# Adding four expert rows per token: engine sums against accumulating loads in a two-layer Mamba/attention + mixture-of-experts kernel

## The reference

```
xn = layernorm(x)                                   # layer 0
x  = x + ssd_block(xn) + moe(xn, 16 experts, top 4) + shared_expert(xn)
xn = layernorm(x)                                   # layer 1
x  = x + spike_attention(xn) + moe(xn, 8 experts, top 2)
```

## Time and profile before

| what | us |
|---|---|
| median of three runs | 2404.99 |
| the profiled execution, its own time | 2406.89 |
| its span in the trace | 2405.1 |
| bridge, first load issued to last normalized group | 1693.9 to 1796.2 |
| busy in the span: PE, DVE, ACT, POOL | 2187.2, 1595.0, 1190.7, 1435.2 |

### The profile page before, as it was taken

The page is one execution under the profiler, slowest core; times in us unless marked ns, Lnnn a source line. Parts: engine busy times, 40 slices in busy tenths (PEclk is TensorE's granted clock), DMA queues, the critical chain, the costliest instruction groups (busy, mean ns, idle before and its releaser), DMA issues. The chain is left out here.

```text
span 2405.1 us, 40728 instructions
## 1 busy us (share of the span) xinstructions
PE 2187.2 (91%) x12292; PEld 1586.7 (66%) x12292; DVE 1595.0 (66%) x3484; ACT 1190.7 (50%) x2677; POOL 1435.2 (60%) x1278
## 2 busy tenths in 40 slices
PE   4787999999999999999999989999288879999997
PEld 2455777777777777777777767777144656666665
DVE  4747888888888888888888845666687742222222
ACT  2356777777777777777777722222132341111111
POOL 1224777777777777777777756777643214444443
PEclk9898999999999999999999999999689899999999
DMA  7926454545545455454544448664540046222221
GB/s 255 359 83 146 139 151 132 152 139 151 149 132 156 136 154 145 133 156 139 153 143 132 141 139 278 191 218 150 202 157 1 1 166 173 46 44 45 45 43 20
DMA packets 195651, 330.34 MB, mean 137 GB/s; under 512 B 49267, under 2 KB 137588, under 8 KB 195188
## 3 DMA queue, kind: packets, MB, share of 16 engines
q1 hardware_dynamic: 139044, 233.43, 32.8%
q0 software_dynamic: 26880, 53.64, 8.8%
q10 hardware_dynamic: 29520, 40.66, 5.4%
HBM read 240.72 MB, written 87.84 MB: 137 GB/s over the span
## 5 line engine op out<-in xcount | busy, mean ns | idle before, releaser
L1006 DVE SCALAR_TENSOR_TENSOR m_cv<-m_hp,conv,m_cv 128x256 f32<-128x256 f32 x864 | 417.0, 483 | 112.2 <-ACT m_cv L905 91.0
L1397 PE MATMUL e_u<-wup,e_xgT 128*128 x1152 | 421.4, 499 | 9.0 <-issue 4.9
L1335 ACT ACTIVATE e_sil<-e_u 128x128 f32<-128x128 f32 (+1 forms) x216 | 82.9, 384 | 551.5 <-PE e_u L1397 524.5
L832 POOL TENSOR_TENSOR m_er<-m_er,m_cT 128x1024 f32<-128x1024 f32 x128 | 302.2, 2361 | 44.1 <-DVE m_ar L1013 44.1
L943 ACT ACTIVATE m_ar<-m_ar,m_ta 128x128 f32<-128x128 f32 x1024 | 318.7, 390 | 0.8
L1094 PE MATMUL m_hp<-xnT,wpj 128*128 128x259 f32 x1152 | 304.3, 387 | 7.8 <-PEq L144 4.5
L1397 PEld LDWEIGHTS e_u<-wup,e_xgT 128*128 128x128 f32 x1152 | 203.1, 191 | 141.3 <-issue 130.3
L1102 PE MATMUL m_gp<-xnT,wpj 128*128 128x256 f32 x1024 | 269.1, 385 | 11.2 <-ACT m_gT L923 11.2
L1094 PEld LDWEIGHTS m_hp<-xnT,wpj 128*128 128x128 f32 x1152 | 214.2, 192 | 68.8 <-issue 27.1
L1292 POOL DMA_INDIRECT out<-e_y,target x72 | 113.0, 1570 | 228.7 <-DVE e_y L1366 192.9
L839 POOL TENSOR_TENSOR m_hdd<-m_hdt,m_tb 128x512 f32<-128x512 f32 x128 | 131.0, 1043 | 193.8 <-DVE m_hdt L1021 193.8
(11 more groups left out here) (305 smaller groups left out, 3965.8 us busy)
## 6 DMA issues: line engine op xcount, KB each, us to landing
m_ar<-acum_rows_dram SPq DMA_DIRECT2D x512, 128.0 KB
m_er<-eacum_rows_dram SPq DMA_DIRECT2D x128, 512.0 KB
rows_by_slot<-blank_rows ACTq DMA_DIRECT2D x1, 18576.0 KB, 79.1
e_xg<-rows_by_slot ACTq DMA_DIRECT2D x132, 129.0 KB
m_xrow<-xn_rows SPq DMA_DIRECT2D x32, 512.0 KB
b_work<-y_rows SPq DMA_DIRECT2D x16, 1024.0 KB, 7.0
wup<-in_w SPq DMA_DIRECT2D x8, 1024.0 KB
wpj<-in_w_proj SPq DMA_DIRECT2D x1, 4352.0 KB, 24.4
```

What stands on the lines that cost most here:

```text
L832: g.tensor_tensor(er[:, t], er[:, t], middle(cT[:, t * P:(t + 1) * P], HQ), ALU.mult).then_inc(scaled.sem, 1)
L1006: v_.scalar_tensor_tensor(o, hp[n % 2][:, j:j + BLK], conv[:, c, j:j + 1], o, ALU.mult, ALU.add).then_inc(tapped.sem, 1)
L1397: ins = nc.tensor.matmul(u_ps[a.slot(2)][b][:, 0:width], xgT[:, a.slot(2), c, :], wup[:, c, ds(e * (2 * f) + b * width, width)], start=c = ...
```

## The change

The four rows are no longer loaded beside the stream and summed. GpSimd issues, for each group and each of the four choices, one DMA that reads that choice's rows (128 partitions x 4 pieces of 1 KB) and adds them into `xs` in SBUF as it lands. The four loads of a group follow each other, each waiting for the one before; groups are staggered, so that up to four groups are in progress. The sums on POOL (L1611, L1613), the addition on DVE (L1801) and SP's loads (L1582) are gone; DVE waits for the four landings of a group instead. The zeroing of `cmp` and the index tiles stand after the 32 loads in POOL's stream.

```diff
-        yg = work[:].rearrange("p (r t k d) -> p r t k d", r=2, t=BIG, k=K0)
...
-        s_yg = [sem(f"b_experts{n}") for n in range(4)]
+        s_yg = [sem(f"b_experts_added{n}") for n in range(NG)]
...
             @block.sync
             def _(sp):
-                def y_half(h):
-                    g, half = divmod(h, 2)
-                    if g >= 2:
-                        sp.wait_ge(s_x, g - 1)
-                    sp.dma_start(yg[:, g % 2, half * 2:half * 2 + 2].rearrange("p t k d -> p t (k d)"),
-                                 tokens(by_token, g * BIG + half * 2, 2)).then_inc(s_yg[h % 4], 16)
-
-                for h in range(4):
-                    y_half(h)
                 for g in range(NG):
-                    if g + 2 < NG:
-                        y_half(2 * g + 4)
-                        y_half(2 * g + 5)
                     sp.wait_ge(s_xn, g + 1)
...
             @block.gpsimd
-                for h in range(2 * NG):
-                    g, half = divmod(h, 2)
-                    pool.wait_ge(s_yg[h % 4], (h // 4 + 1) * 16)
-                    a = yg[:, g % 2, half * 2:half * 2 + 2]
-                    g_.tensor_tensor(a[:, :, 0:2, :], a[:, :, 0:2, :], a[:, :, 2:4, :], ALU.add).then_inc(s_pc, 1)
-                    pool.wait_ge(s_pc, h + 1)
-                    g_.tensor_tensor(a[:, :, 0, :], a[:, :, 0, :], a[:, :, 1, :], ALU.add).then_inc(s_ys, 1)
-                    if h == 1:
-                        (iotas and casts of tokid, ji, slot_row)
-                pool.wait_ge(s_x, NG - 1)
+                def add_choice(g, j):
+                    if j:
+                        pool.wait_ge(s_yg[g], 16 * j)
+                    pool.dma_start(xs[:, g * BIG:(g + 1) * BIG, :], tokens(by_token, g * BIG, BIG)[:, :, j * D:(j + 1) * D],
+                                   accum_op=ALU.add).then_inc(s_yg[g], 16)
+
+                for n in range(NG + K0 - 1):
+                    for j in range(K0 - 1, -1, -1):
+                        if 0 <= n - j < NG:
+                            add_choice(n - j, j)
                 g_.memset(cmp, 0.0).then_inc(s_cz, 1)
+                (iotas and casts of tokid, ji, slot_row)
...
             @block.vector
-                        dve.wait_ge(s_ys, 2 * s.n + 2)
-                        v.tensor_tensor(xs[:, at, :], xs[:, at, :], yg[:, s.n % 2, :, 0, :], ALU.add).then_inc(s_x, 1)
-                        dve.wait_ge(s_x, s.n + 1)
+                        dve.wait_ge(s_yg[s.n], 16 * K0)
```

More of the change, by code:

```diff
@@ L1543, in bridge_phase @@
         plane = lambda r, g: raw[:, r, ds(g * GT, GT)] if r < R - KD else xnT[:, r - (R - KD), ds(g * GT, GT)]
-        s_yg = [sem(f"b_experts{n}") for n in range(4)]
-        s_ys, s_pc = sem("b_y_summed"), sem("b_y_pairs")
-        s_x, s_lst, s_small, s_std0, s_rstd, s_xn = (sem("b_" + n) for n in (
-            "stream", "row_stats", "row_moments", "row_std", "row_rstd", "xn_done"))
+        s_yg = [sem(f"b_experts_added{n}") for n in range(NG)]
+        s_lst, s_small, s_std0, s_rstd, s_xn = (sem("b_" + n) for n in (
+            "row_stats", "row_moments", "row_std", "row_rstd", "xn_done"))
         s_row = [sem(f"b_rows_stored{n}") for n in range(XN)]
@@ new lines, in _ @@
+                g_.memset(cmp, 0.0).then_inc(s_cz, 1)
+                g_.iota(tokid[:], pattern=[[P, T]], base=-S, channel_multiplier=1).then_inc(s_iota, 1)
+                g_.iota(ji[:], pattern=[[1, 1]], base=0, channel_multiplier=1).then_inc(s_iota, 1)
+                g_.iota(slot_row_i[:], pattern=[[1, P]], base=0, channel_multiplier=0).then_inc(s_iota, 1)
+                pool.wait_ge(s_iota, 3)
+                g_.tensor_copy(token_f[:], tokid[:]).then_inc(s_turn, 1)
+                g_.tensor_copy(jf[:], ji[:]).then_inc(s_turn, 1)
@@ L1624, in _ @@
+                g_.tensor_copy(slot_row[:], slot_row_i[:]).then_inc(s_turn, 1)
                 g_.memset(mask[:], 1.0).then_inc(s_m, 1)
```

## The result

The changed kernel takes 2420.7 us (median of 8 runs, 2414.8 to 2424.0) against 2405.9 us for the kernel before in the same comparison. The ratio is 1.0057, 95% interval 1.0043 to 1.0072: slower by 0.6%, about 14 us. I had forecast slower, but by 87 us.

A forecast was written before the change was run, and what follows sets the result against it. Bound: the feed chain load, sum, normalize, up to the eighth group's addition. Last landing 1877.8 instead of 1791.5 us, +86.3; PE -1.1 and +2.2; sum +87.4 on the profiled 2406.9 us; against the median, 2492 us. Range 2425 to 2532.

The forecast's parts named there:

- What bounds the bridge: Between 1693.9 and 1797 us: the feed chain of load, sum, normalize sets the time, and PE comes last.
- GpSimd's price of an issue: POOL's own time for each new accumulating load: 0.40 us plus 1024 reads at 4.6 ns, 5.1 us.
- The DMA engines' price: Engine time per added 1 KB packet: 0.105 to 0.154 us, so 3.4 to 4.9 us per load.
- The pace: Spacing of the 32 loads: set by POOL's issue, 5.1 + 0.3 us, so 5.4 us per load.
- rival A: Bridge loads paced by the DMA engines at 3.4 to 4.9 us each: total about 2426 to 2474 us, chance 0.26.
- what I cost at nothing: Zeroing of `cmp` and index tiles behind POOL's loads, SP's row stores, DVE's slow tiny operations: no effect on the total.
- Three lone round trips: At the ends of the load stream: three loads are waited for alone, 3 x (5.1 + 4) = 27.3 us.
- PE's terms: PE at the eighth group: no longer late, -1.1 us; lower clock after gaps in transposes and projection, +2.2 us.
- The work moved behind the loads: Zeroing of `cmp` (1.8 us) and index tiles on POOL: covered before routing begins; without cover about 4 us.
- Rival D: Bridge loads: only the second read costs, 0.085 us per KB, 2.7 us per load; total 2403 us, chance 0.04.

## Why the prediction was wrong, point by point

* **What bounds the bridge:** right. All the loss lies between the first load and the eighth group's statistics. From there to the first gather of the last phase it is 0.9 us less than before: 1.2 us more to the kept scores, and 2.1 us less behind them, where I had expected no change.
* **GpSimd's price of an issue, 5.1 us: this step failed.** The trace after has 1.28 us for 512 pieces. I had read the surplus of the indirect adding DMA over the indirect plain one, 0.59 us, as 4.6 ns for each additional read, and then scaled it by the number of pieces. Measured on direct loads, 128 adding pieces cost 0.865 us, 512 cost 1.282 us, and the plain load, which goes out as 128 packets, 0.748 us: 1.1 ns per piece and a fixed part of about 0.7 us. The bounds of my sum went from 1.57 to 6.3 us, and the truth lay below the lower one. An indirect DMA's time was not a floor for a direct one.
* **The DMA engines' price, 0.105 to 0.154 us per added KB:** as the time of a packet right at its lower end, 0.104 us; as a pace too high. I multiplied it by the 32 pieces of an engine and got 3.4 us, as if the packets stood one behind the other. They overlap: full engines deliver a load in 2.7 us at a share of 1.23. The higher row held one DMA alone, with its start and its end; with a filled queue the row from the middle of a DMA was the nearer one.
* **The pace:** I took GpSimd's 5.4 us per load; the engines' 3.1 us (12.4 us per group over 4) decided. This was rival A, to which I gave 0.26. Its formula with the measured numbers, 29 x 3.1 + 3 x (1.28 + 1.2 + 3.1), gives 106.6 us against the 110.3 measured. Its lower end stood at 3.4 us per load, hence 2426 us, and that was also the lower end of my range; the overlap of the packets is what carried the time below it. That 3.4 and 3.1 are so near is partly luck. The overlap was left out, 0.7 us too much, and so were the row stores on the same engines, some 0.3 us too little: under "what I cost at nothing" I had asked only whether anybody waits for them.
* **Three lone round trips:** right in place. The first load alone took 6.3 us to landing, and the last pair shows 8.8 us between two issues (1788.23 to 1797.02). The size was 6.1 to 8.8 us (the last load is issued at 1797.02 and used at 1803.10) instead of 9.1.
* **PE's terms, -1.1 and +2.2 us:** the sum is right by luck. From the statistics of the eighth group to its kept scores it is 22.7 us (1803.10 to 1825.81) against 21.5 us before (1791.49 to 1813.03), +1.2 for +1.1 forecast. But PE was as late as before: it took up the group 5.9 us after the statistics began in both kernels. Now it first turned an earlier group's scores (L1661, at 1808.08), which waited for DVE's copy L1814, and that stands behind the normalization in DVE's stream. And the lower clock cost 1.2 us instead of 2.2: the eight transposes took 1.91 us instead of 1.04, the projection 2.21 instead of 1.88.
* **The work moved behind the loads** (zeroing, index tiles): covered, as said. It ended on POOL by 1802 us, and routing began at 1827 us.
* **Rival D, twice the plain price, chance 0.04:** its price was the true one. Full engines need 0.083 us per added KB, 2.7 us per load, which is D's 2 x 0.042. I had put it aside because the earlier trace rows gave 0.105 to 0.154 us, but these are times of single packets and not what full engines deliver. What it lacked are the row stores, which make the pace 3.1 us, and longer round trips at both ends, so that no change became +14 us. "Collectives: The Full Stack" in the Trainium skill, section on the bandwidth ceiling, says of a collective's reduce step that the add costs no cycles and the second source read halves the rate. The rates here agree with a halving; that a second read is the reason, no row shows.

What stays open: how the 12.7 us divide between pace and ends. At a pace of 3.1 us 32 loads are 99 us, so some 11 us are round trips at both ends. Reordering the start gave 2.6 us of them back in one profile, and the end was not tried alone. The share of the row stores in the pace is an estimate; no run left them out.

## What to carry to other kernels

An adding DMA is not a free sum. It moved the four-row sum from GpSimd and VectorE to the 16 DMA engines, where an added KB costs twice a plain one, and they became the bound. Before work is given to a DMA, divide its bytes by the rate that full engines deliver for that kind of packet, add whatever else uses the engines, and compare that with the spacing of the consumer. Packet times multiplied up overstate it when the share is over 1. The kernel that adds one row in four this way, where the DMA engines had room, is 0.6% faster than the kernel before. And an engine that issues dependent loads should have other loads between them, because everything else in its stream stands behind the wait.

## What the runs showed of the hardware

A direct adding DMA from GpSimd, device memory into SBUF in fp32: 1.28 us of GpSimd for 512 pieces of 1 KB, 0.865 us for 128 pieces of 4 KB; the plain one 0.748 us. A plain load whose 512 pieces of 1 KB land side by side in fours went out as 128 packets of 4 KB, the adding one as 512 packets. On the DMA engines a packet takes 0.104 us for an added piece of 1 KB and 0.33 us for one of 4 KB, against 0.042 us per plain KB. Full of adding packets, the 16 engines deliver 196 GB/s with pieces of 1 KB and 211 GB/s with 4 KB. An adding load of 512 KB in pieces of 1 KB lands 5.9 us after its issue at the least, a plain one 3.7 us. Adding packets overlap each other on an engine (a share of 1.18 over 30 us with no other transfer), and row stores overlap them too, so that the summed share reads 1.21.
